# Degrees of a graph stack: row sums on VectorE in place of a product on TensorE, with a new order of the stages

## What is computed

```
L0:  h = (1 + eps) * x + adj^T x ;  relu(h W1 + b1) W2 + b2, masked
L1:  degree = adj.sum(-1)
     relu(concat(x, (adj^T x) / degree) W^T + b)
L2:  adj_self = adj + I ; d = rowsum(adj_self) ** -0.5 (inf -> 0)
     (adj_self * d_i * d_j) (x W) + bias
L3:  for all i, j: h_ij = relu(x_i W1a + x_j W1b + b1)
     y_ij = layernorm(h_ij W2 + b2) * gamma + beta ; out_i = sum_j adj_ij y_ij
```

## Time and profile before

| | |
|---|---|
| runs of the kernel before | 457.12, 459.3, 460.74 us; median 459.3 |
| profiled execution | span 459.2 us (its own time is not listed beside it; the span lies 0.1 us under the median of the runs) |
| PE busy | 440.2 us (96%) |
| PE weight loads busy | 414.6 us (90%) |
| DVE busy | 416.2 us (91%) |
| ACT busy | 386.5 us (84%) |
| POOL busy | 354.0 us (77%) |
| mean granted TensorE clock | 0.987 of full speed |

### The profile page before, as it was taken

One profiled execution on the slowest core, in us unless ns is written; L12 is line 12 of the kernel. 1 busy time (PEld: TensorE's weight loads), 2 busy tenths in 40 slices (PEclk: granted clock), 3 DMA queues, 4 the chain that ended last, 5 costly groups with the idle time before them and its releaser, 6 DMA issues. The chain is left out here.

```text
span 459.2 us, 14175 instructions
## 1 busy us (share of the span) xinstructions
PE 440.2 (96%) x3420; PEld 414.6 (90%) x3453; DVE 416.2 (91%) x1523; ACT 386.5 (84%) x1003; POOL 354.0 (77%) x651
## 2 busy tenths in 40 slices
PE   8699989999999999999999999999999999999993
PEld 3599989999999999889998999999999999999991
DVE  6989999999999999996898898899889888989975
ACT  2368979999999899998788888888888888888874
POOL 4569979999999899756677787777768676868762
PEclk9889999999999999999999999999999999999997
DMA  7134344445444652233313222232223131313111
GB/s 221 41 83 131 95 139 161 153 151 178 154 148 156 221 190 77 76 109 121 122 55 99 69 74 80 69 85 63 91 60 94 51 103 51 103 51 86 37 46 49
DMA packets 50939, 47.60 MB, mean 104 GB/s; under 512 B 5584, under 2 KB 42576, under 8 KB 50896
## 3 DMA queue, kind: packets, MB, share of 16 engines
q1 hardware_dynamic: 49760, 46.45, 33.2%
q10 hardware_dynamic: 1136, 0.66, 0.5%
HBM read 28.22 MB, written 18.87 MB: 103 GB/s over the span
## 5 line engine op out<-in xcount | busy, mean ns | idle before, releaser
L1593 PEld LDWEIGHTS bank<-w2c,hE 128*128 128x128 f32 x512 | 67.3, 192 | 2.4
L1593 PE MATMUL bank<-w2c,hE 128*128 128x128 f32 x512 | 67.5, 275 | 0.2
L905 ACT ACTIVATE hE<-bank,front 128x512 f32<-128x512 f32 x64 | 44.2, 691 | 7.6 <-PE bank L1574 7.4
L927 ACT ACTIVATE sqE<-bank 128x512 f32<-128x512 f32 x63 | 37.7, 599 | 12.8 <-PE bank L1593 12.3
L1237 DVE TENSOR_REDUCE ssum<-sqE 128x4 f32<-128x512 f32 x63 | 42.6, 676 | 4.3 <-ACT sqE L927 2.9
L706 POOL TENSOR_TENSOR gHl<-gH,gHu 128x512 fp32r<-128x512 f32 x32 | 41.0, 1283 | 5.6 <-ACT gHu L879 5.6
L1104 DVE BATCH_NORM_STATS2 stats<-t 128x6 f32<-128x128 f32 x192 | 44.4, 272 | 1.0 <-issue 1.0
L1262 DVE TENSOR_TENSOR ym<-bank,wE 128x512 f32<-128x512 f32 x64 | 43.2, 681 | 1.6 <-POOL wE L755 0.3
L722 POOL TENSOR_TENSOR half<-ym 128x512 f32<-128x512 f32 x31 | 39.5, 1273 | 3.3 <-DVE ym L1262 3.1
L1591 PE MATMUL bank<-bias,ones_b 128*128 128x512 bf16 x92 | 35.0, 380 | 0.7 <-DVE ym L1262 0.6
L1593 PEld LDWEIGHTS bank<-w2c,hC 128*128 128x128 f32 x256 | 33.6, 192 | 1.3
(11 more groups left out here) (191 smaller groups left out, 1624.6 us busy)
## 6 DMA issues: line engine op xcount, KB each, us to landing
hh_scratch<-hh SPq DMA_DIRECT2D x32, 256.0 KB, 2.2
gH<-hh_scratch SPq DMA_DIRECT2D x32, 256.0 KB, 2.8
A<-adj_groups SPq DMA_DIRECT2D x32, 128.0 KB, 2.1
res_scratch<-res SPq DMA_DIRECT2D x32, 128.0 KB, 2.1
gRES<-res_scratch SPq DMA_DIRECT2D x32, 128.0 KB, 2.5
AT<-adjT_groups SPq DMA_DIRECT2D x31, 128.0 KB, 2.3
out<-y SPq DMA_DIRECT2D x30, 128.0 KB, 1.9
X<-x_groups SPq DMA_DIRECT2D x29, 128.0 KB, 2.2
```

Of the source, the lines that this page charges most:

```text
L905: nc.scalar.activation(hE[g][:, :], HE_ps, ACT.Relu, bias=C["L3_b1"]).then_inc(b[f"hE{g}_ready"], 1)
L927: nc.scalar.activation(sqE[g][:, :, :], YE_ps[g], ACT.Square).then_inc(b[f"sqE{g}_ready"], 1)
L1593: last = nc.tensor.matmul(ps[:, i, :], hidden[:, i * P:(i + 1) * P], w2c[:, :], start=False, stop=i == tiles - 1)
```

## The change

`count_row`, `keep_sums`, `find_holes` (POOL) and `keep_counts` go, with the tile `beta1` and the bank that held the sums. In their place: DVE `sum_rows` sums the rows of `A` into `deg`, one reduction of 128x2 from 128x256; ACT `spread_degrees` makes `bdeg` from `beta` with the degree as the scale, two operations on 128x128; DVE `find_holes` makes `hole` and `found` in two operations on 128x2. The next load of `A` waits for `deg_ready` as well, that of `AT` no longer for the product. The nominal moments of all dense stages, of `T3` and of `FIRST` (now for 8 first units, not 6) are new.

```diff
-        sums = sb("sums", [P, SLOTS, GROUP, P + 1])
-        bdeg, deg = sums[:, :, :, 0:P], sums[:, :, :, P]
+        bdeg = sb("bdeg", [P, SLOTS, GROUP, P])
+        deg = sb("deg", [P, SLOTS, GROUP])
...
             def next_at(k, r, n):
                 if not is_last(r):
-                    sp.wait_ge(s["sums_psum"], n)
                     sp.wait_ge(s["ai_done"], n)
...
             def next_a(k, r, n):
                 if not is_last(r):
                     sp.wait_ge(s["xT_psum"], n)
+                    sp.wait_ge(s["deg_ready"], n)
...
-            def find_holes(k, r, n):
-                pool.wait_ge(s_setp, 3)
-                pool.wait_ge(s["sums_ready"], n)
-                nc.gpsimd.tensor_scalar(hole[:, k, :], deg[:, k, :], -1.0, None, ALU.is_equal).then_inc(s["hole_found"], 1)
-
-            def keep_counts(k, r, n):
-                pool.wait_ge(s["hole_found"], n)
-                nc.gpsimd.tensor_tensor(found[:, bass.ds(SLOTS * r + k, 1), :].rearrange("p o c -> p (o c)"), deg[:, k, :], hole[:, k, :], ALU.add).then_inc(s["found_ready"], 1)
...
-            def keep_sums(k, r, n):
-
+            def spread_degrees(k, r, n):
+
+                if isinstance(r, int) and r == 0:
+                    act.wait_ge(s_const, 16)
                 wait_past(act, s["res_ready"], n - SLOTS)
-                wait_past(act, s["found_ready"], n - SLOTS)
-                wait_past(act, s["rdeg_ready"], n - SLOTS)
-                act.wait_ge(s["sums_psum"], n)
-                nc.scalar.activation(sums[:, k, :, :], sums_ps, ACT.Copy).then_inc(s["sums_ready"], 1)
+                act.wait_ge(s["deg_ready"], n)
+                for g in range(GROUP):
+                    last = nc.scalar.activation(bdeg[:, k, g, :], C["beta"], ACT.Copy, scale=deg[:, k, g:g + 1])
+                last.then_inc(s["bdeg_ready"], 1)
...
+            def sum_rows(k, r, n):
+
+                dve.wait_ge(a_loaded[k], 16 * r + 16)
+                wait_past(dve, s["bdeg_ready"], n - SLOTS)
+                wait_past(dve, s["found_ready"], n - SLOTS)
+                nc.vector.tensor_reduce(deg[:, k, :], A[k][:, :, :], AX.X, ALU.add).then_inc(s["deg_ready"], 1)
+
             def degrees(k, r, n):
 
-                dve.wait_ge(s["sums_ready"], n)
+                dve.wait_ge(s["deg_ready"], n)
...
+            def find_holes(k, r, n):
+
+                dve.wait_ge(s["deg_ready"], n)
+                wait_past(dve, s["dis_ready"], n - SLOTS)
+                nc.vector.tensor_scalar(hole[:, k, :], deg[:, k, :], -1.0, None, ALU.is_equal)
+                nc.vector.scalar_tensor_tensor(found[:, bass.ds(SLOTS * r + k, 1), :].rearrange("p o c -> p (o c)"), deg[:, k, :], -1.0, deg[:, k, :],
+                                               ALU.is_equal, ALU.add).then_inc(s["found_ready"], 1)
...
-            dense_stages = [(5.48, find_flaws), (14.94, sum0), (15.62, stats0), (16.57, var0), (19.4, rstd0), (20.43, apply0), (26.49, degrees), (27.21, sum1a),
-                     (28.48, sum1b), (30.57, stats1), (31.6, inverse_root), (31.93, var1), (32.89, rstd1), (39.51, sum2),
-                     (41.27, stats2), (42.85, var2), (44.78, rstd2)]
+            dense_stages = [(0.19, find_flaws), (15.39, sum0), (15.93, stats0), (16.82, var0), (20.27, rstd0), (21.14, apply0), (15.66, sum_rows), (25.81, degrees), (26.75, find_holes), (27.63, sum1a),
+                     (28.42, sum1b), (30.07, stats1), (29.5, inverse_root), (32.41, var1), (33.49, rstd1), (39.92, sum2),
+                     (41.08, stats2), (43.12, var2), (45.4, rstd2)]
...
-            def count_row(k, r, n):
-
-                wait_past(pe, s["sums_ready"], n - 1)
-                pe.wait_ge(at_loaded[k], 16 * r + 16)
-                for g in range(GROUP):
-                    last = nc.tensor.matmul(sums_ps[:, g, :], AT[k][:, g, :], beta1[:, :], start=True, stop=True)
-                last.then_inc(s["sums_psum"], 1)
```

More of the change, by code:

```diff
@@ L213, in gnn_stack @@
         hh_ps = results(bank[6], 2 * P)
-        COUNTS = GROUP * (P + 1)
+        COUNTS = GROUP * P
         off_ps, graph_ps = bank[7][:, COUNTS:COUNTS + B], bank[7][:, COUNTS + B:COUNTS + 2 * B]
@@ L278, in gnn_stack @@
         at_loaded = [sem(f"at_loaded{k}") for k in K4]
-        names = ["a0_ready", "ai_done", "ad_ready", "sums_psum", "sums_ready", "hole_found", "found_ready", "rdeg_ready", "rsq_ready", "dis0_done", "dis_ready",
+        names = ["a0_ready", "ai_done", "ad_ready", "deg_ready", "bdeg_ready", "found_ready", "rdeg_ready", "rsq_ready", "dis0_done", "dis_ready",
                  "ot_ready", "unlike_done", "hT_psum", "hT_ready", "u_psum", "rT_ready", "y_psum",
@@ L364, in wait_past @@
                 engine.wait_ge(semaphore, n)
[L368 removed]
[4 rows of a table removed]
[L373 removed]
+        T3 = {"idx": 6.14, "rows": 15.37, "V": 17.4, "cols": 20.38, "g0": 17.76, "g1": 22.88, "gc": 20.69, "m0": 23.11, "m1": 24.97, "mc": 24.68,
[4 rows of a table added]
         AGES = 4
         START3, EARLY, CATCH = 216.0, 5.0, 25.0
[L376 to L380, removed]
[7 rows of a table removed]
[L388 to L389 removed]
[4 rows of a table removed]
[L394 to L396 removed]
[5 rows of a table removed]
[L402 removed]
[9 rows of a table removed]
[L412 to L414 removed]
@@ L569, in store @@
                 sp.dma_start(out_d[bass.ds(u * GROUP, GROUP), :, :].rearrange("g p f -> p g f"), (gRES if at_end(u) else y4)[q][:, :, :]).then_inc(out_stored[q], 16)
-            dense_stages = [(24.2, next_a), (25.28, next_x), (25.66, next_at), (26.27, keep(ot, ot_s, "ot_ready", ot_stored)),
-                     (58.51, keep(res, res_s, "res_ready", stored)), (69.62, keep(hh, hh_s, "hh_ready", stored))]
+            dense_stages = [(19.18, next_a), (26.61, next_x), (11.6, next_at), (28.78, keep(ot, ot_s, "ot_ready", ot_stored)),
+                     (56.53, keep(res, res_s, "res_ready", stored)), (50.43, keep(hh, hh_s, "hh_ready", stored))]
             edge_stages = [(("idx", 0.5), next_ot), (("spl", "hs", 1.5), next_h), (("rs", 0.8), next_res), (("app", 1), store)]
@@ L696, in residual @@
                 pool.wait_ge(s["x3_ready"], n)
-                pool.wait_ge(s["sums_ready"], n)
+                pool.wait_ge(s["bdeg_ready"], n)
                 pool.wait_ge(stored[k], 32 * r + 1)
@@ L766, in out_shift @@
                 nc.gpsimd.tensor_tensor(oshift[q][:, :], omean[q][:, :], orstd[q][:, :], ALU.mult).then_inc(b["oshift_ready"], 1)
-            dense_stages = [(3.9, add_scaled), (20.34, add_identity), (20.37, mark_edges), (26.78, find_holes), (28.51, keep_counts), (33.57, negate_mean),
-                     (34.21, make_shift), (34.26, guard_root), (35.9, scale_adj), (37.09, add_bias2), (48.2, residual)]
+            dense_stages = [(3.52, add_scaled), (13.59, add_identity), (10.28, mark_edges), (30.04, negate_mean),
+                     (31.6, make_shift), (29.93, guard_root), (30.96, scale_adj), (33.54, add_bias2), (44.75, residual)]
             edge_stages = [("spl", split_lower), ("hs", add_ends), ("a1", add_halves), ("a2", add_pairs), ("gm", times_gamma),
@@ L1097, in _ @@
             dve.wait_ge(s_const, 16)
-            nc.vector.tensor_copy(beta1[:, 0:P], C["beta"])
             def layer_norm(layer):
@@ L1598, in stage @@
                     if isinstance(u, int) and u == 0:
-                        pe.wait_ge(s["z_done"] if g == 0 else s["sums_ready"], GROUPS)
                         pe.wait_ge(s_bias, 3)
+                        if g == 0:
+                            pe.wait_ge(s["z_done"], GROUPS)
                         if g == 1:
@@ L1627, in scatter @@
                 last.then_inc(b["O_psum"], 1)
-            dense_stages = [(5.87, hidden0), (7.19, mlp0a), (12.19, mlp0b), (21.57, count_row), (22.18, turn1), (24.73, project1), (36.61, aggregate2),
-                     (38.48, project2), (49.49, turn3), (54.26, project3)]
+            dense_stages = [(6.86, hidden0), (11.61, mlp0a), (12.35, mlp0b), (21.56, turn1), (24.6, project1), (35.88, aggregate2),
+                     (37.05, project2), (48.45, turn3), (50.04, project3)]
             edge_stages = [("idx", indices), ("rows", start_rows), ("V", place_rows), ("cols", start_columns), ("g0", gather_ell(0)),
```

40 lines of the change are left out of this document (24 added, 16 removed), and 69 rows, old and new, of tables (FIRST, T3).

## The result

The changed kernel takes 492.9 us (median of four runs, 491.16 to 497.06), beside 459.2 for the kernel before on the same chip: a ratio of 1.075, 95% interval 1.069 to 1.082. The forecast was 468 with a range of 450 to 479. The sign was right, and the size was off by a factor of nearly four: 33.7 us lost and not 9.

The account below looks back on a forecast made before the run. PE set the 5.52 us dense step, with DVE next; the bound was to pass to DVE at 5.87 us, losing 0.35 a group. 26 x 0.35 = 9.1 us and nothing for the rest gave 468 us, range 450 to 479.

Parts of the forecast that it names:

- Waits and loads: SP's loads and their waits: next_a's added wait costs nothing, and next_at moving ahead of loads of X costs nothing.
- DVE's 5.87: Dense loop: DVE's period per group after the change, 5.43 + 0.44 + 0.09 idle - 0.09 = 5.87 us, becoming the bound.
- floor of 5.07: Dense loop, PE: removing count_row's four matmuls, 0.45 us, lowers PE's floor per group from 5.52 to 5.07 us.
- 464 to 473: Whole kernel: the main forecast's time in us, with DVE at 5.7 to 6.0 us a group; chance 0.42.
- The collisions: Dense loop: two DVE lines waiting for POOL cost 0.66 us a group, relieved by 0.09; nothing taken for new operations.
- the rule cited there: Dense loop: GpSimd contends with VectorE instructions in a two-port mode or with two SBUF inputs; found would then collide.
- a step under 5.5: Dense loop, sign of being wrong: a group step under 5.5 us would mean DVE's collisions were slack and not cost.
- rival 1: Dense loop: collisions mostly vanish, DVE at 5.30 to 5.40 us a group, 453 to 455 us in all; chance 0.15.
- The clock: Dense loop, sign of being wrong: the granted clock falls because PE now pauses; 85% busy was not expected to do so.
- Start: Before the dense loop: a third find_flaws and sum_rows come in front; nothing taken, up to 3 us either way.
- Edge part: Edge loop: same instructions in a new order; nothing taken for 32 units, range 6 us loss to 2 us gain.
- exposed `w`: Edge loop: DVE stands still 0.54 us a unit before the weighing, waiting for POOL's w; expected to fit idle time.

Follow-up runs that it names:

- e1: Changed kernel with only the load of X moved ahead of the load of A in SP's queue: 476.7 us, ratio 1.039.
- e5: Changed kernel with the load of X directly behind that of A, ahead of the stores of hh and res: 478.0 us, ratio 1.040.
- e4: Kernel before with only the load of X moved behind the stores and the next group's load of A: 540.8 us, ratio 1.180.
- e7: e3 with the two small operations (find_holes, keep_counts) back on POOL: 467.3 us, ratio 1.017.
- e3: Kernel before with the changed operations, but the old order on every engine and the old T3 and FIRST: 472.9 us, ratio 1.030.
- e10: e7 with the reduction of A moved in DVE's queue behind find_flaws of the next group: 459.9 us, ratio 1.003.
- e11: e3 with the reduction moved behind find_flaws, the two small operations staying on VectorE: 466.6 us, ratio 1.018.
- e6: e3 with the reduction done twice, the first into a tile that nobody reads: 474.6 us, ratio 1.033.
- e12: Changed kernel with the load of X as in e1 and the reduction at its moment in e10, here still ahead of find_flaws: 473.2 us, ratio 1.031.

## Why the prediction was wrong

The step that failed is the last sentence of "Waits and loads": "I cost it at nothing; a load late by one place would show as DMA waits of POOL." That part looked at `next_a` and `next_at` and never priced `next_x`, which the diff moves from directly behind `next_a` to behind the stores of `hh` and `res`. The trace of before had the terms. SP's issues stand 0.45 to 0.6 us apart, so three of them take some 1.6; a load of 128 KB lands after 2.1 to 2.5 us; and the load of `A` waits for `turn1`. On PE the new order puts only `project3` between `hidden0` and `turn1`, and with their times of before (0.44, 0.87 and 0.83 us) that is 2.1. Walking the new order with these numbers gives 2.1 + 1.6 + 2.1 to 2.5 = 5.8 to 6.2 us a step, level with DVE's 5.87 or above it, and with nothing to spare for a load that lands late. The runs showed 6.55 on the mean. The load was late for PE, and not for POOL. e1 and e5 show that this is worth 15 to 16 of the 33.7 us; e4 shows that such a load slows the kernel before too.

- *PE.* Right: the four matmuls went, and their floor of 5.07 is real, since e7 ran on it for three steps. Over a whole loop no version of the change came down to it.
- *DVE.* Right as a step, tested alone by e3: 5.80 us against 5.87. That its 472.9 us lie in the forecast's 464 to 473 is in part luck: the 13.7 us lost are more than 26 x 0.28 = 7.3, and 6.7 of them lie in the seven steps of groups 5 to 12, which the sum took for steps like the others. The reduction (0.326 against 0.32) was right. The two small operations were sized at 0.12 and are worth 5.6 to 6.7 us of the whole, 0.22 to 0.26 us a group, when they stand where they collide (e3 against e7, e10 against e11). The collisions, taken as an unchanged 0.66 less 0.09, were in other places, with nearly the same sum. `found`, which by the rule cited there might collide for its two inputs, never took longer (a slot of 0.070 to 0.073 in e3), but it follows directly on a `hole` that has just waited, so this does not test the rule.
- *That DVE's full queue is a cost and not slack* held only in part. e6 added 0.32 us a group for 1.7 us in all. The prediction said that a step under 5.5 would mean that collisions were slack. e10 has 5.38, but with the small pair on POOL; with all changed operations it is 5.59 in e11 and 5.49 in e12. So the mechanism of rival 1 exists in part, but the order of this change doesn't reach it.
- *ACT.* 5.40 us a group was forecast, and ACT has 83.94 / 100 x 6.55 = 5.50 in the changed kernel. It was not the bound in any run, although at 97.60 in e10 it is close.
- *The clock.* The prediction counted a fall of the granted clock in the dense loop as a sign of being wrong. It came, from 70.0 to 73.4 us, after a pause of 2.90 us, and not in the stretch from 75 to 175 us. 3.4 us at half clock are at most 1.7 us of PE's work, by this estimate a small part of the loss.
- *Start.* Nothing was taken, with up to 3 us either way; it cost 3.6. The profile after shows PE waiting at 17.03 us for `apply0`, which stands on DVE behind the preparation of the constants:

```profile
17.03 0.48 PE L1489 MATMUL bank<-ident,x 128*128 128x128 f32 x1 [3.92 <-DVE x L1127]
```

```profile
13.55 0.72 DVE L1055 CAST bias<-back 1x256 bf16<-1x256 f32 x1
...
16.37 0.60 DVE L1127 TENSOR_SCALAR x<-t,mv,rstd 128x128 f32<-128x128 f32 x2
```

  In the kernel before, `apply0` went ahead of those constants.
- *The ends of the loop* had no term at all. The 5.52 of the kernel before is a mean from group 5 to 31 that was taken for a stretch without gaps; in fact its steps are 4.44 to 7.28 up to group 12, with a pause of PE of 1.53 us at 65.56. Groups 5 to 12 and 27 to 31 cost 12.5 us in the changed kernel, and still 9.2 in e12.
- *Edge part.* Right: nothing was taken, -1.3 us was measured. The exposed `w` is there as forecast (DVE's `ym` waits 13.7 us in all for it) and costs nothing.
- *Spans.* The prediction used the span of 459.2 and the median of 459.3 alike. In the other profiled executions the span is 1.7 to 2.2 us under the run's own time, so the execution profiled before was probably near 461; this decided nothing.
- *Rivals.* Each varied the computing engines. None had a DMA in it, so the range could hold only what those engines can do.

The 33.7 us, then, by three kernels with the same operations: 13.7 for the changed operations in the old order (e3), 16.2 for the place of the load of `X` (the changed kernel against e1), and 3.8 for the rest of the new order (e1 against e3). With the reduction moved in both orders (e12 against e11) the rest of the new order is 6.7. By the starts of the groups, that is +4.9 at the start, +1.7 in groups 5 to 12 and +3.5 in groups 27 to 31, against -1.5 in the middle and -2.8 in the edge part.

## What to carry to other kernels

When a change brings a new order, write the old and the new order of every queue side by side, SP's above all, and walk one period with issue spacing, landing time and the wait at the head; a load that moved behind a store is a term of the sum even if its own conditions come early. When no engine is full after a change, look for the load that lands just ahead of its reader in every period; a load with time to spare also takes up its own late landings. An engine that is 98% busy beside one that it collides with is not simply full: move an operation in its queue before moving it to another engine, since here the place of one reduction was worth 5 to 7 us, most of the 26 x 0.32 = 8.3 us of its slot.

## What the runs showed of the hardware

- An operation on VectorE with two SBUF inputs that starts inside one of GpSimd's ends 0.28 us after that one's end (started at 137.56 against an end at 138.06 in e3, 83.24 against 83.68 in e10), unless its own 0.42 us take it further; the other way round, GpSimd's 0.73 us became 0.98 (e7). A reduction with one input is not delayed (0.41 us inside `xb` in e6).
- An operation on 128x2 elements with a single tensor input, `hole`, collides too: 365 ns on the mean in e3 where 127 is the shortest, and it ends 0.03 us after GpSimd's `add_scaled` (e11). So the number of SBUF inputs alone doesn't tell which operations collide.
- The same program can leave one pace for another within a run: 5.08 us a group and then 5.8 (e7). In the second pace `sum1b` starts behind GpSimd's `xb` in 13 of 15 groups, in the first in none.
- A load of 128 KB on SP's queue landed 2.1 to 2.5 us after its issue in most groups, but 3.4 to 4.7 in some (3.39 at 100.22 in the kernel before, 4.20 at 88.07 in the changed one).
